# Cross-attention's division moved from VectorE to GpSimd, and the last transpose of shifts of each pair of heads placed three key blocks later

## What is computed

```python
x = x + attn(layernorm(x), Wq, Wk, Wv, Wo)            # 16 heads of 16, ALiBi slopes, causal
x = x + xattn(layernorm(x), ctx, Wq, bq, ...)         # 16 heads of 64, then + residual and a layernorm
x = x + fp8_product(layernorm(x), kernel, scales, bias)

# xattn, for each head:
scores = einsum('bqhd,bkhd->bhqk', q, k) / 8
attn = softmax(scores)
out = einsum('bhqk,bkhd->bqhd', attn, v)              # then @ Wo + bo + residual
```

## Time and profile before

| | us |
|---|---|
| three runs | 2104.93, 2118.03, 2148.95 |
| their median | 2118.03 |
| the profiled execution | 2105.83 |
| its span, first to last instruction | 2104.0 |

### The profile page before, as it was taken

The page is one execution under the profiler, slowest core; times in us unless marked ns, Lnnn a source line. Parts: engine busy times, 40 slices in busy tenths (PEclk is TensorE's granted clock), DMA queues, the critical chain, the costliest instruction groups (busy, mean ns, idle before and its releaser), DMA issues.

```text
span 2104.0 us, 30713 instructions
## 1 busy us (share of the span) xinstructions
PE 1869.7 (89%) x11354; PEld 995.6 (47%) x11354; DVE 1359.7 (65%) x2479; ACT 896.9 (43%) x1794; POOL 982.9 (47%) x808
## 2 busy tenths in 40 slices
PE   7788988889988998899999899999999999898772
PEld 3444444444444544445545455545555545454331
DVE  4667676776722647756746756755765764776888
ACT  2235566666654232333343344343444433344432
POOL 1000000000001445657777777866866876785654
PEclk9769999999989899999999999999999999999986
DMA  4222102240010000000000000000000000000001
GB/s 103 34 33 32 23 11 32 32 83 16 2 50 30 8 1 9 1 1 11 1 1 11 1 1 11 1 1 11 1 1 3 2 1 3 1 5 26 1 21 40
DMA packets 27741, 34.55 MB, mean 16 GB/s; under 512 B 3986, under 2 KB 25811, under 8 KB 25939
## 3 DMA queue, kind: packets, MB, share of 16 engines
q1 hardware_dynamic: 27592, 32.59, 8.6%
HBM read 14.99 MB, written 4.19 MB: 9 GB/s over the span
## 4 chain that ended last, share of the span: by engine, by line
PE 72%; DVE 18%; ACT 5%; issue 3%; SPq 1%; DMA 1%; POOL 1%; ACTq 0%; POOLq 0%; DVEq 0%
PE psum L869 14%; PE psum L884 13%; DVE maxima L1135 8%; PE psum L857 6%; PE psum L777 6%; PE psum L691 5%; PE psum L752 4%; PE psum L873 4%; PE psum L725 4%; ACT weights_room L967 4%; PE psum L907 3%; PE psum L845 3%; DVE parts_room L1223 2%; DVE parts_room L1218 2%; PE psum L789 2%
## 5 line engine op out<-in xcount | busy, mean ns | idle before, releaser
L1135 DVE TENSOR_REDUCE maxima<-psum 128x1 f32<-128x400 f32 (+5 forms) x1664 | 876.4, 581 | 333.8 <-PE psum L857 180.8
L666 POOL TENSOR_TENSOR parts_room<-parts_room,weights_room 128x512 f32<-128x512 f32 (+1 forms) x558 | 708.8, 1301 | 236.1 <-ACT weights_room L1025 233.1
L1025 ACT ACTIVATE weights_room<-psum 128x512 f32<-128x512 f32 (+1 forms) x694 | 369.9, 597 | 519.5 <-PE psum L873 517.5
L967 ACT ACTIVATE weights_room<-psum 128x512 f32<-128x512 f32 (+3 forms) x640 | 297.8, 535 | 226.4 <-PE psum L752 121.5
L1337 POOL TENSOR_SCALAR rstd<-meanvar 128x2 f32<-128x2 f32 (+1 forms) x24 | 7.2, 301 | 693.4 <-DVE meanvar L1085 693.3
L869 PE MATMUL psum<-stack_room,k_hi 64*128 64x512 f32 (+1 forms) x1664 | 309.1, 411 | 14.5 <-ACT weights_room L1025 14.5
L857 PE MATMUL psum<-k_hi,stack_room 64*128 64x400 f32 (+1 forms) x1024 | 261.8, 401 | 53.7 <-DVE maxima L1135 51.4
L857 PEld LDWEIGHTS psum<-k_hi,stack_room 64*128 64x128 f32 x1024 | 147.4, 187 | 225.6 <-issue 115.1
L752 PE MATMUL psum<-stack_room,stack_room 51*128 51x512 f32 (+3 forms) x640 | 194.8, 436 | 43.3 <-ACT weights_room L967 41.6
L869 PEld LDWEIGHTS psum<-stack_room,k_hi 64*128 64x128 f32 (+1 forms) x1664 | 170.2, 184 | 64.8 <-ACT weights_room L1025 28.8
L873 PE MATMUL psum<-shifts,parts_room 64*128 64x512 f32 (+1 forms) x832 | 195.7, 398 | 0.0
(11 more groups left out here) (124 smaller groups left out, 1817.1 us busy)
## 6 DMA issues: line engine op xcount, KB each, us to landing
stack_room<-parts_room SPq DMA_DIRECT2D x96, 128.0 KB
x_block<-x_dram SPq DMA_DIRECT2D x8, 512.0 KB, 4.7
x_middle<-x_block SPq DMA_DIRECT2D x4, 512.0 KB, 3.1
x_block<-x_middle SPq DMA_DIRECT2D x4, 512.0 KB, 5.4
out_dram<-x_block SPq DMA_DIRECT2D x8, 256.0 KB, 2.1
parts_room<-ctx_dram SPq DMA_DIRECT2D x1, 1536.0 KB
stack_room<-shift_rows SPq DMA_DIRECT2D x64, 2.0 KB
parts_room<-wq_dram SPq DMA_DIRECT2D x8, 128.0 KB, 2.2
```

What stands on the lines that cost most here:

```text
L666: engine.tensor_tensor(sum_[:kw, :], old[:kw, :], weights[u % NP_WEIGHTS][:kw, :], ALU.add) \
L967: engine.activation(w_self[s % NW][:, m, 0:n], self_scores[(HP * s + m) % SELF_SCORES][:, 0:n], ACT.Exp, scale=SELF_SCALE).then_inc(exp_do ...
L1025: engine.activation(weights[u % NP_WEIGHTS][:kw, :], pair_scores[u % NSCORES][:kw, :], ACT.Exp, scale=CROSS_SCALE).then_inc(pair_exp, 1)
L1135: engine.tensor_reduce(maxima[:, p % 2, i // TB, n, i % TB, ch:ch + 1], bank_of(use + n)[:, 0:real - k0], AX.X, ALU.max) \
```

## The change

The division is taken out of DVE's program and put into POOL's, with the same two waits. `PROJECT_LAG` grows by one step. In both attentions the last `rows` of a sweep 1 is no longer put right behind the last `negate` but handed to `after(ROWS_LAG, ...)`, which puts it three steps later, in the sweep 2 that is then running. In `pair_sweep1` the edit is the same. Four calls keep the old order with `waits=True`: those whose rows are needed at once.

```diff
-SUMS_LAG, PROJECT_LAG = 4, TB + 3
+SUMS_LAG, PROJECT_LAG = 4, TB + 4
...
-    def sweep1(self, p, blocks=range(NB)):
+    def sweep1(self, p, blocks=range(NB), waits=False):
...
-        return steps + [(0, what) for _, what in made]
+        last = [(0, what) for _, what in made]
+
+        return steps + (last if waits else [(0, lambda: self.after(ROWS_LAG, last[-1][1]))])
...
-        self.interleave([(w, step, 0) for w, step in self.sweep1(0, early)], value_steps, start=0.0)
+        self.interleave([(w, step, 0) for w, step in self.sweep1(0, early, waits=True)], value_steps, start=0.0)
...
-        self.interleave([m for m in first if m[2] in early], self.sweep1(0, late), start=0.0)
+        self.interleave([m for m in first if m[2] in early], self.sweep1(0, late, waits=True), start=0.0)
...
-        now(self.pair_queries(0) + self.pair_sweep1(0, [0]))
+        now(self.pair_queries(0) + self.pair_sweep1(0, [0], waits=True))
...
-            elif kind == "pair_divide":
-                n_block = pair_finish_no[at]
-                dve.wait_ge(evicted, n_block + 1)
-                dve.wait_ge(inverted, TB * (n_block + 1))
-                engine.tensor_tensor(o_pair[n_block % 2], o_pair[n_block % 2], pair_recip, ALU.mult) \
-                    .then_inc(divided, 1)
...
+            elif kind == "pair_divide":
+                n_block = pair_finish_no[at]
+                pool.wait_ge(evicted, n_block + 1)
+                pool.wait_ge(inverted, TB * (n_block + 1))
+                engine.tensor_tensor(o_pair[n_block % 2], o_pair[n_block % 2], pair_recip, ALU.mult) \
+                    .then_inc(divided, 1)
```

More of the change, by code:

```diff
@@ L193, in sweep2, with pair_sweep1 @@
         return steps
-    def pair_sweep1(self, p, blocks=range(NB)):
+    def pair_sweep1(self, p, blocks=range(NB), waits=False):
         steps, made = [], []
```

## The result

The changed kernel takes 2168.0 us in the median of four runs (2148.6 to 2191.9); the kernel before takes 2111.5 us in four runs, one more than the three shown above. The ratio is 1.025, with a 95% interval of 1.013 to 1.037. A second set of six runs of the same changed kernel gave 1.023 (1.018 to 1.028). So it is slower, by 2% or a little more; both intervals leave open whether it is more than 2%.

The account below looks back on a forecast made before the run. PE was taken as the bound. New waits less DVE's holds +20, clock +17, rows -6, SP's queue +8, last pair -3: +36 on 2105.8 gives 2142; half of the runs' 12 us added gives 2148 us, range 2102 to 2182.

Parts of the forecast that it names:

- the forecast's own range: Whole kernel: 2132 to 2165 us around the likeliest time of 2148 us; chance 0.45.
- DVE's holds go: Pairs 2 to 6 of the second attention: DVE's long divisions, which make PE wait, disappear; -32 us.
- PE waits for POOL: Projection, second attention: PE waits for the division queued behind POOL's additions; +52 us.
- The clock: PE's clock falls behind the new waits at the projection: 12 falls of 1.4 us, +17 us.
- Rows later: Transposes: PE's waits for DVE's `negate` shrink when rows of shifts come later; -6 us.
- SP's queue at pair 5: Self-attention pair 5: last rows' DMAs queue behind the load, ACT's copy waits, then PE, and the clock falls; +8 us.
- The last pair: Last pair: DVE loses three or four divisions of 0.69 us, some tail steps move by one call; -3 us.
- The clock holds: Rival: no fall of the clock behind the new waits; 2125 or 2137 us, chance 0.22.
- POOL is in time: Rival, at the projection: the division is done when PE needs it, so the change is faster; 2065 to 2077 us, chance 0.09.
- Lateness grows: Rival: POOL's lateness grows with each division and the clock falls at every wait; about 2200 us, chance 0.11.
- It nearly cancels: Rival: waits half as long (26 instead of 52 us), clock falls half as often; 2107 to 2119 us, chance 0.13.

Follow-up runs that it names:

- proj_later: The changed kernel with the projection two key blocks later in pairs 0 to 6: 2077.5 us, ratio 0.979 to the kernel before.
- div_only: The changed kernel with every row of shifts back in its old place, the division staying on POOL: 2187.4 us, ratio 1.029.
- best2: The changed kernel with projection two key blocks later in pairs 0 to 6, last pair as before, rows colliding with the load put back: 2069.9 us, ratio 0.980.
- tail_lag: The changed kernel with the lag back at TB + 3 in the last pair alone, division still on POOL: last stretch 147.7 us in one run.
- after_again: The changed kernel once more, unaltered, for a second trace: 2173.0 us, ratio 1.023 to the kernel before.

## Why the prediction was right, and where it was not

The measured median of 2168.0 us lies in the range (2102 to 2182), 20 above the likeliest time and 3 above the forecast's own range (2132 to 2165). Within 2% was given the larger chance (0.57, slower 0.35); the ratio came out at 1.025, with an interval that holds both. On the profiled execution the sum said 2142, and it was 2148.6. The mechanism was the one predicted. That the sum came so near is in part luck. In pairs 1 to 5 its terms were +44 for the waits, +14 for the clock and -24.5 for the holds, together +33.5; measured are about +39, +23 and -30, together the 31.4 us above: the clock cost more than I took, the waits a little less, and the holds gave back more. In the second trace of the same kernel, with more falls of the clock, these pairs and all that comes before them were longer, and it took 2195.7 us. Point by point:

- **DVE's holds go** (-32, of which -24.5 in pairs 1 to 5): right. Pairs 1 to 5 of before are 30 us above five times the 156.2 us of `proj_later`, and no hold is left.
- **PE waits for POOL** (+52; 8.8 us a pair, 3.1 at two blocks, 1.8 and less at the others): right. 57.6 us in 29 waits, 2.75 and 3.2 us at two blocks of a pair, 8.6 us a pair. For pair 0 I had put 1 us; its four projections wait 4.4 us, 0.3 once and 1.4 three times. Per pair only 7.8 us of idle time are added, since part of PE's other idle time goes.
- **Skill and row.** The Trainium skill (GPSIMD Engine Reference, "Elementwise — side-by-side cycle accounting") measures a float32 addition of 2048 columns on GpSimd at 1.96 times VectorE's time, and sends elementwise work to VectorE. Here the division of 512 columns took 1.26 us on POOL against 0.68 undisturbed on DVE, 1.85 times. The advice held for the place that the change chose, and not with the later projection, where POOL's slower division costs PE nothing.
- **The clock** (+17 for 12 falls of 1.4): right in kind, mis-sized. In the first trace the number of falls was right, one behind each of the twelve longer waits of pairs 1 to 6, but pairs 1 to 5 lost 23 us by their ten, 2.3 a fall. I had priced a fall by pair 3's excess over pair 1, where the fall stood in 3.4 us of half clock; here five of the twelve last twice as long. In the second trace the price was near mine, 1.7 us, and the number was wrong: it fell behind the waits of 1.2 to 1.4 us too, four times a pair, 6.8 us. I had left those out because a PE that was busy for 2.69 of 4 us had kept its clock; that row didn't carry over. The median of the first four runs is 19 us above their profiled run; whether this is the reason can't be told, since only the profiled runs show the clock by pairs.
- **Rows later** (-6): under-sized on the waits, 9.9 us less at L745 (`div_only` against the changed kernel), all of them ahead of or in pair 0. What that saves in time isn't shown: pair 0 is only 1.6 us shorter (187.15 against 188.75), and ahead of it the clock hides it. In pairs 1 to 5 it brings nothing.
- **SP's queue at pair 5** (+8): right in place and cause. ACT waits for a landing and PE waits 5.7 us for ACT from 473 us on; the wait is absent in `div_only` and `best2`. The fall of the clock was priced too low, at 1.4: from 470 to 498 us the mean clock is 0.70, against 1.00 before, which is some 8 us. That the whole stretch ahead of the first projection is only 3.4 us longer is no evidence against it, as the clock there moves it by 35 us between traces of one kernel.
- **The last pair** (-3): wrong in sign, +3.2. I had taken the lost divisions on DVE as the larger part and the moved steps as the smaller; `tail_lag` shows a gain of 1.5 at most from the one and a loss of 4.0 from the other.
- **The rivals.** "The clock holds" was wrong. "POOL is in time" was wrong for this kernel and right once PE comes later; its 2065 to 2077 us, worked out for that case, is what the later projection gives (0.979 of the 2105.8 or 2118.0 that it started from is 2062 or 2074). "Lateness grows" was wrong in its first half, since the waits are the same in all pairs, and right in its second: the clock did fall at every wait of pairs 1 to 5 in three traces, and its time of 2200 is near the longest runs (2192 and 2196). "It nearly cancels" was wrong: the waits are 57.6 us in total, and not half of 52.

## What to carry to other kernels

An engine with a free quarter of its time can still be behind at one place of its list: before moving work to it, look at what it is doing when the waiting engine arrives there, and move the reader back along with the work. On the engine that bounds this kernel a wait of 1.2 to 3.2 us cost its length and, where the clock fell behind it, 1.7 or 3.4 us more. So price a wait with the clock loss behind it, and take that from several traces rather than from one. When a step is moved "later", look at every queue that it passes, and at the last iteration, where moving a step has no cover.

## What the hardware did that I had not expected

- The same waits do not make the same falls. Behind the waits of 2.75 to 3.2 us in pairs 1 to 6 the clock fell every time, in all five traces with the whole division on POOL and the projection at its old place. Behind those of 1.2 to 1.4 us it did not fall in pairs 1 to 6 of the first trace of the changed kernel, and fell at each one of pairs 1 to 5 in those of `after_again`, `div_only` and `tail_lag`. A pair takes 168.7 us in the one case and 170.7 in the other. What decides between the two isn't shown.
- Behind waits of 1.7 to 2.2 us it fell six times in twelve.
- DVE and POOL do not hold each other up alike here. A division on DVE takes up to 7.0 us beside POOL's additions in three kernels, while on POOL, in the changed kernel, it took 1.3 us at most in pairs 0 to 5 and 1.74 at most from then on.
